# Unread products of the identity with itself in eleven waits of TensorE

## The chip, the cores and the metric

One core of one Trainium2 chip runs the whole program. The metric is the device time in microseconds, as the median of several executions; lower is better. The reference is a function of 34 arrays; all arithmetic is done on the core.

## The reference, cut to what matters

2048 tokens of width 256 pass through two residual blocks. The first is a gated linear-recurrence attention followed by an MLP of width 1024; the second is a mixture of 8 experts (two per token) with a shared expert of width 704.

```python
x = x + layernorm(attn(layernorm(x), ...))
x = x + layernorm(ffn(layernorm(x), ...))

def attn(x, ...):
    h = layernorm(x)
    x_conv = silu(causal_depthwise_conv(h, 4 taps))
    q, k = l2norm(h @ Wq), l2norm(h @ Wk)          # by heads of 16
    v = layernorm(h @ Wv)
    i_gate, gamma = sigmoid(x_conv @ Wig + big), sigmoid(x_conv @ Wg + bg)
    mem = scan(mem = gamma * mem + i_gate * k * v)    # over the tokens
    out = layernorm(layernorm(mem) * q) * gnw + gnb
    out = out * sigmoid(x_conv @ Wog + bog)
    h = x + out @ Wo
    h2 = layernorm(h)
    return h + (silu(h2 @ Wgate) * (h2 @ Wval)) @ Wout
```

Everything is fp32; the products of the MLPs are formed from high and low parts of each operand, three products each (`mm3`).

## The kernel before

The tokens are cut into four blocks (`TILES`) of four tiles of 128. Each block goes through the attention steps of the list `ATTENTION`, through the MLP (`mup`, `mdn`) and the shared expert (`hid`, `sdn`); the routed experts come at the end in 39 groups, then the final sum. Each engine has its own stream of instructions. `steps(engine)` merges two lists for it: `ORDER`, the steps of the MLPs and the router, and the attention steps, each of which stands before the element of `ORDER` whose number `PLACE[engine]` gives. The order is thus written out by hand, and each engine runs it in program order, with semaphores for what one engine needs from another. The attention of block b+1 is laid between the MLP steps of block b.

Two stretches have no MLP products beside them. One is the attention of block 0: all its steps stand ahead of the first `mup`. The other is the stop between the MLP of block 0 and that of block 1: after the last `mdn` of block 0 come `og`, `wo`, `ht` (of block 2, one block ahead), `xt`, `h2`, `route` and `logit`, and only then the first `mup` of block 1.

The steps of TensorE that the change touches, as (stage, block, part):

- `ut`: eight transposes of the update u to the layout by features. It waits for the vector engine's L1294.
- `mt`: eight products with the centring matrix, which also turn the scanned memory back to tokens. It waits for the scan, L1305.
- `g` part 2: the output gate's four products of 512 columns. It waits until the normalised memory has left `p_main` (L1333). ScalarE reads its result at L607.
- `og`: eight transposes of the output `HN`. It waits for L1336 and for the output gate.
- `wo`: the eight products with Wo. It waits for L1349, which itself follows ScalarE's L621 on the result of `og`.
- `ht` of the next block: eight transposes of the normalised input, after L1355 has read the result of `wo` from `p_main`.
- `h2`: eight transposes of the input of the MLP, two for each of four tiles that ScalarE writes at L632.
- `q` part 0 of the next block: four products with the weights of q, k and v. It waits for L637 on the result of `h2`.
- `xt`: eight transposes of the router's input, two for each of four tiles that ScalarE writes at L658.

`p_main` is banks 0 and 1 of PSUM, which these steps share one after the other. Bank 2 is the first bank of the first of two pairs (`p_pair`) that hold the halves of `mup` and `hid`. In the first block's attention `q` of block 0 uses it too (`q_banks`).

In fp32 one product on TensorE is recorded as two MATMULs with two weight loads; a transpose is recorded as one.

Of the kernel before, what the change touches and what calls it, by code (L numbers as in the profile page):

```python
# [11 lines left out]
P = 128  # L12
# [55 lines left out]
def _order():  # L68
# [89 lines left out]
    ],  # L158
}


def steps(engine):
# [9 lines left out]
def build(nc, x, wq, wk, wv, wig, wog, wo, wg, wgate, wval, wout, vecs, headvecs, router, sup, sdn, rup, rdn, out):  # L172
    ctx = ExitStack()
    with ctx:
# [3 lines left out]
        def sb(name, shape, dt=F32):  # L178
            return ctx.enter_context(nc.sbuf_tensor(name, shape, dt))

        psum = ctx.enter_context(nc.psum_tensor("psum", [P, 8, 512], F32))
# [51 lines left out]
        with ExitStack() as first_names:  # L233
            wr, wg16, wmean, _, wgx = (first_names.enter_context(nc.sbuf_tensor(k, s, F32)) for k, s in (
                ("wr", [P, C, RP]), ("wg16", [P, C, HEADS]), ("wmean", [P, C, HEADS]),
                ("under_rupr", [P, E * C * GU - C * (RP + 2 * HEADS)]), ("wgx", [P, C, D])))
# [7 lines left out]
        ident = sb("ident", [P, P])  # L244
# [497 lines left out]
        def _(pe):  # L742
# [6 lines left out]
            def to_features(dst, src, nj, ready=None, before=0):  # L749

                for j in range(nj):
                    if ready is not None:
                        pe.wait_ge(ready, before + j + 1)
                    for c in range(C):
                        last = nc.tensor.transpose(dst[:, c, j * P:(j + 1) * P], src(j)[:, c * P:(c + 1) * P], ident[:, :])  # L755
                return last
# [33 lines left out]
            def at(stage, b, m):  # L790
                nj, old, new = TILES[b], START[b], START[b + 1]
                tb = nj * P
                if (stage, m) == ("ht", 0):
                    if b > 0:
                        pe.wait_ge(hr_ready, b)
                    to_features(p_main, lambda j: QKV[:, j, 0:D], nj, hn_ready, old).then_inc(ht_psum, 1)
                if stage == "q" and m < nj:
# [12 lines left out]
                    for part, cols in ((0, slice(0, 2 * D)), (1, slice(2 * D, 3 * D))):  # L810
                        for c in range(C):
                            last = nc.tensor.matmul(q_banks(b, m)[:, part, 0:cols.stop - cols.start], HT[:, c, tok], WQKV[:, c, cols],  # L812
                                                    start=c == 0, stop=c == C - 1)
                    last.then_inc(qkv_psum, 1)
                if stage == "g":
# [8 lines left out]
                    for o in range(C):  # L824
                        if m == 1:
                            pe.wait_ge(gate_ready, C * 3 * b + o + 1)
                        for c in range(C):
                            if m == 1:
                                last = nc.tensor.matmul(p_main[:, o, 0:tb], wgx[:, c, o * P:(o + 1) * P], XC[:, c, 0:tb],  # L829
                                                        start=c == 0, stop=c == C - 1)  # L830
                            else:
                                cols = slice(m // 2 * D + o * P, m // 2 * D + (o + 1) * P)
                                last = nc.tensor.matmul(p_main[:, o, 0:tb], GW[:, c, cols], XC[:, c, 0:tb],  # L833
                                                        start=c == 0, stop=c == C - 1)
# [19 lines left out]
                if stage == "wo":  # L854
# [3 lines left out]
                    for j in range(nj):  # L858
                        cols = slice(j * P, (j + 1) * P)
                        for c in range(C):  # L860
                            last = nc.tensor.matmul(p_main[:, j // 2, (j % 2) * D:(j % 2 + 1) * D], OG[:, c, cols], WO[:, c, :],  # L861
                                                    start=c == 0, stop=c == C - 1)
# [44 lines left out]
                if stage == "rank":  # L907
# [6 lines left out]
                                     stop=False, skip_group_check=True)  # L914
# [15 lines left out]
            for name, b, m in steps("pe"):  # L930
                at(name, b, m)
# [619 lines left out]
```

## Time and profile before

| | |
|---|---|
| time, median of 3 runs | 600.58 us (600.44, 600.58, 602.94) |
| profiled execution, first to last instruction | 603.1 us |
| mean granted clock of TensorE | 0.933 |
| TensorE, MATMUL busy | 518.9 us, 86% of the span, 2408 instructions |
| VectorE, ScalarE, GpSimd busy | 394.2, 263.7, 109.5 us |

The profile's table of forty slices gives the busy share of each engine and the granted clock of TensorE in tenths. The chain of waits is followed back from the last instruction, and says which engine's work set the end. The timeline of an engine lists its instructions, with the idle time before each group and the instruction that ended it in square brackets. Times on the timeline are counted from the first instruction. The table by windows gives the granted clock of chosen stretches: 1.00 is 2.4 GHz and 0.50 is 1.2 GHz. The span is 0.2 us longer than the slowest of the three timed runs and 2.5 us longer than their median.

### The profile page before, as it was taken

Reading aid. Unit: us, or ns where it says so; the run is one execution under the profiler, and the core shown is the slowest. Engines: PE = TensorE matmul, PEld = TensorE weight load, DVE = VectorE, ACT = ScalarE, POOL = GpSimd, SP = SyncE. Lnnn points to the kernel's source line nnn. Section 1 sums busy time; section 2 is a strip of 40 time slices with the busy share of each in tenths; the row PEclk is TensorE's granted clock in tenths of the full one; section 3 lists DMA queues with packets and bytes.
Section 4 is the critical chain, followed back from the end, with each engine's and each line's share of the span. In section 5 each row is a group of like instructions: output and inputs, shape, how many; then the busy total and the mean of one; then the engine's idle time right before and its main releaser. Section 6 shows DMA issues by size and latency. Waiting matters only on the chain.

```text
span 603.1 us, 7985 instructions
## 1 busy us (share of the span) xinstructions
PE 518.9 (86%) x2408; PEld 407.6 (68%) x2408; DVE 394.2 (65%) x1159; ACT 263.7 (44%) x469; POOL 109.5 (18%) x133
## 2 busy tenths in 40 slices
PE   2845358999569999999999998999997899999981
PEld 1413234677446587886677786788876799999871
DVE  6786643879865798875497774434657666767236
ACT  4721444425374424276631444311344456666204
POOL 1510003200002323002204000050004034444300
PEclk9985679999959999999999999999989999999986
DMA  8950000001110002021001011010129234444364
GB/s 292 380 178 15 20 2 0 1 2 35 35 35 1 0 19 89 4 66 36 1 5 67 1 35 36 0 70 2 36 71 281 77 94 119 136 124 117 106 226 139
DMA packets 29547, 44.52 MB, mean 74 GB/s; under 512 B 3083, under 2 KB 24203, under 8 KB 29163
## 3 DMA queue, kind: packets, MB, share of 16 engines
q1 hardware_dynamic: 24515, 33.07, 17.8%
q0 software_dynamic: 3408, 9.38, 4.2%
q10 hardware_dynamic: 1584, 1.57, 0.9%
q8 instruction: 21, 0.34, 0.2%
q14 instruction: 19, 0.16, 0.1%
HBM read 27.67 MB, written 16.34 MB: 73 GB/s over the span
## 4 chain that ended last, share of the span: by engine, by line
PE 71%; DVE 15%; ACT 7%; DMA 4%; issue 2%; POOL 0%; ACTq 0%; POOLq 0%; SPq 0%; DVEq 0%
PE psum L786 14%; PE psum L745 12%; PE psum L746 11%; PE psum L747 11%; PE psum L812 5%; PE psum L755 4%; PE psum L833 3%; DMA RDNR<-rdn 2%; PE psum L861 2%; DVE XC L1244 2%; PE psum L829 2%; PE psum L847 2%; PE psum L986 1%; PE psum L956 1%; PE psum L939 1%
## 5 line engine op out<-in xcount | busy, mean ns | idle before, releaser
L650 ACT ACTIVATE SM<-psum 128x512 f32<-128x512 f32 (+1 forms) x56 | 33.2, 594 | 123.0 <-PE psum L747 99.7
L1369 DVE TENSOR_TENSOR SM<-SM,psum 128x512 f32<-128x512 f32 (+1 forms) x56 | 38.2, 683 | 56.4 <-ACT SM L650 56.3
L526 POOL DMA_INDIRECT x_dispatched<-XN,dest x32 | 32.5, 1017 | 159.2 <-DVE XN L1437 150.7
L786 PE MATMUL psum<-WOU,SM 128*128 128x256 f32 x256 | 60.2, 380 | 0.0
L786 PEld LDWEIGHTS psum<-WOU,SM 128*128 128x128 f32 x256 | 48.3, 190 | 10.7 <-issue 2.4
L517 POOL TENSOR_TENSOR OG<-QKV,hvec 128x256 f32<-128x256 f32 x16 | 13.4, 836 | 228.1 <-ACT IG L592 214.5
L812 PE MATMUL psum<-WQKV,HT 128*128 128x512 f32 (+1 forms) x128 | 47.5, 520 | 6.5 <-ACT QKV L585 3.1
L535 POOL DMA_INDIRECT y_routed<-GO,g_dest x39 | 37.8, 968 | 67.8 <-ACT GO L720 67.5
L786 PE MATMUL psum<-SDN,SM 128*128 128x256 f32 (+1 forms) x192 | 44.8, 382 | 0.0
L812 PEld LDWEIGHTS psum<-WQKV,HT 128*128 128x128 f32 x128 | 24.9, 201 | 28.0 <-issue 21.6
L786 PEld LDWEIGHTS psum<-SDN,SM 128*128 128x128 f32 (+1 forms) x192 | 35.9, 189 | 6.5 <-issue 1.3
L833 PE MATMUL psum<-XC,GW 128*128 128x512 f32 x64 | 31.6, 641 | 8.1 <-DVE HN L1333 5.9
L745 PE MATMUL psum<-H2H,wgtH 128*128 128x512 f32 x64 | 30.8, 481 | 0.0
L745 PE MATMUL psum<-RUPH,GXH 128*128 x78 | 28.9, 371 | 1.9 <-DVE GXL L1451 1.9
L755 PE MATMUL psum<-ident,QKV 128*128 128x128 f32 x64 | 11.2, 331 | 22.3 <-ACT QKV L563 9.2
L833 PEld LDWEIGHTS psum<-XC,GW 128*128 128x128 f32 x64 | 13.0, 206 | 22.5 <-issue 13.1
L745 PE MATMUL psum<-XTH,supH 128*128 128x512 f32 x66 | 27.8, 421 | 0.0
L1451 DVE TENSOR_TENSOR GXL<-psum,GXH 128x256 fp32r<-128x256 f32 x39 | 16.5, 424 | 15.7 <-ACT GXH L707 15.7
L747 PE MATMUL psum<-XTH,supL 128*128 128x512 f32 x66 | 26.2, 396 | 0.0
L746 PE MATMUL psum<-XTL,supH 128*128 128x512 f32 x66 | 26.0, 394 | 0.0
L746 PE MATMUL psum<-H2L,wgtH 128*128 128x512 f32 x64 | 25.8, 403 | 0.0
L747 PE MATMUL psum<-H2H,wgtL 128*128 128x512 f32 x64 | 25.8, 403 | 0.0
(295 smaller groups left out, 1301.4 us busy)
## 6 DMA issues: line engine op xcount, KB each, us to landing
XG<-x_dispatched SPq DMA_DIRECT2D x39, 130.0 KB, 2.7
YF<-y_routed SPq DMA_DIRECT2D x4, 1024.0 KB, 9.0
RUPR<-rup SPq DMA_DIRECT2D x1, 2816.0 KB
X<-x SPq DMA_DIRECT2D x4, 512.0 KB, 6.8
x_after_attention<-X SPq DMA_DIRECT2D x4, 512.0 KB, 2.9
QKV<-x ACTq DMA_DIRECT2D x3, 512.0 KB, 3.5
y_shared<-SH SPq DMA_DIRECT2D x3, 512.0 KB, 2.9
SHF<-y_shared SPq DMA_DIRECT2D x1, 1536.0 KB, 18.9
```

Of the source, the lines that this page charges most:

```text
L526: nc.gpsimd.indirect_dma_start(XD[:, :], bass.IndirectOffsetOnAxis(dest[:, i, old + j:old + j + 1], 0), XN[:, j, :], None).then_inc(dispat ...
L535: nc.gpsimd.indirect_dma_start(YD[:, :], bass.IndirectOffsetOnAxis(g_dest[:, i:i + 1], 0), GO[:, i % ORING, :], None).then_inc(go_kept[i % ...
L650: nc.scalar.activation(SM[0:rows, g % 3, 0:tb], p_pair(n)[0][0:rows, 0:tb], ACT.Silu).then_inc(silu_ready, 1)
L745: nc.tensor.matmul(dst, aH, bH, start=start, stop=False, skip_group_check=shared)
L746: nc.tensor.matmul(dst, aH, bL, start=False, stop=False, skip_group_check=shared)
L747: return nc.tensor.matmul(dst, aL, bH, start=False, stop=stop, skip_group_check=shared)
L755: last = nc.tensor.transpose(dst[:, c, j * P:(j + 1) * P], src(j)[:, c * P:(c + 1) * P], ident[:, :])
L786: last = nc.tensor.matmul(p_down[:, j // 2, (j % 2) * D:(j % 2 + 1) * D], SM[0:rows, g % 3, j * P:(j + 1) * P], weight[0:rows, m, :], star ...
L812: last = nc.tensor.matmul(q_banks(b, m)[:, part, 0:cols.stop - cols.start], HT[:, c, tok], WQKV[:, c, cols], start=c == 0, stop=c == C - 1)
L833: last = nc.tensor.matmul(p_main[:, o, 0:tb], GW[:, c, cols], XC[:, c, 0:tb], start=c == 0, stop=c == C - 1)
L1369: nc.vector.tensor_tensor(SM[0:rows, g % 3, 0:tb], SM[0:rows, g % 3, 0:tb], value_rows(n, rows)[:, 0:tb], ALU.mult).then_inc(hid_ready, 1)
L1451: nc.vector.tensor_tensor(GXL[:, i % 2].rearrange("p c t -> p (c t)"), g_bank(0, i)[:, 0:D], f32(GXH[:, i % 2].rearrange("p c t -> p (c t) ...
```

## The change

A table names eleven steps of TensorE and a count for each. Ahead of the step's own waits and work, TensorE now runs that many products of `ident` with itself, 128 by 128 by 128 in fp32, into the first 128 columns of bank 2. Each of them starts a new accumulation, and nothing reads the result. They wait for nothing. There are 157 of them in all: 115 in the attention of block 0 and its end (`ut`, `mt`, `g` part 2, `og`, `wo`, `ht` of block 1, `h2`, `q` of block 1), and 42 in the stop (`ht` of block 2, `xt`, `h2` of block 1). No other instruction, order or wait is changed.

```diff
+BUSY = {("ut", 0, 0): 17, ("mt", 0, 0): 16, ("g", 0, 2): 24, ("og", 0, 0): 26, ("wo", 0, 0): 9, ("ht", 1, 0): 5, ("h2", 0, 0): 12,
+        ("q", 1, 0): 6, ("ht", 2, 0): 27, ("xt", 0, 0): 8, ("h2", 1, 0): 7}
+
+
 def steps(engine):
 
@@ -790,6 +794,8 @@
             def at(stage, b, m):
                 nj, old, new = TILES[b], START[b], START[b + 1]
                 tb = nj * P
+                for _ in range(BUSY.get((stage, b, m), 0)):
+                    nc.tensor.matmul(psum[:, 2, 0:P], ident[:, :], ident[:, :], start=True, stop=True)
                 if (stage, m) == ("ht", 0):
```

## Rows read from the trace of the kernel before

**Rows 1.** The profile's page: granted clock in forty slices, and the chain by engine.
```profile
PEclk9985679999959999999999999999989999999986
PE 71%; DVE 15%; ACT 7%; DMA 4%; issue 2%; POOL 0%; ACTq 0%; POOLq 0%; SPq 0%; DVEq 0%
```
**Rows 2.** Windows of TensorE: stretch and length, busy (count), granted clock, DMA share, GB/s.
```profile
78.10:84.80 6.70, 2.12 (x13) 1.00 0.01 1
91.70:163.30 71.60, 64.19 (x261) 1.00 0.03 8
163.40:183.80 20.40, 13.05 (x43) 0.50 0.16 52
371.10:375.70 4.60, 1.97 (x16) 1.00 0.32 114
```
**Rows 3.** Timeline of TensorE, block 0: start, length, line, tiles, count, idle before.
```profile
27.50 3.70 PE L833 MATMUL psum<-XC,GW 128*128 128x512 f32 x8 [2.19 <-ACT QKV L585]
...
40.16 1.75 PE L755 MATMUL psum<-ident,QKV 128*128 128x128 f32 x8 [4.54 <-DVE QKV L1294]
45.85 3.78 PE L847 MATMUL psum<-centring,IG 128*128 128x128 f32 x16 [3.94 <-DVE IG L1305]
55.53 6.37 PE L833 MATMUL psum<-XC,GW 128*128 128x512 f32 x8 [5.90 <-DVE HN L1333]
68.61 1.97 PE L755 MATMUL psum<-ident,HN 128*128 128x128 f32 x8 [6.72 <-DVE HN L1336]
72.94 6.19 PE L861 MATMUL psum<-WO,OG 128*128 128x256 f32 x16 [2.35 <-DVE OG L1349]
80.44 1.09 PE L755 MATMUL psum<-ident,QKV 128*128 128x128 f32 x8 [1.31 <-DVE HR L1355]
84.99 2.08 PE L755 MATMUL psum<-ident,HN 128*128 128x128 f32 x8 [3.46 <-ACT HN L632]
88.70 4.28 PE L812 MATMUL psum<-WQKV,HT 128*128 128x512 f32 x8 [1.63 <-ACT GA L637]
```
**Rows 4.** Timeline of TensorE, both clocks: start, length, line, count.
```profile
45.85 2.50 PE L847 MATMUL psum<-centring,IG 128*128 128x128 f32 x10 [3.94 <-DVE IG L1305]
...
106.17 0.58 PE L745 MATMUL psum<-H2H,wgtH 128*128 128x512 f32 x1
...
109.16 3.60 PE L833 MATMUL psum<-XC,GW 128*128 128x512 f32 x8
...
123.98 2.05 PE L847 MATMUL psum<-centring,IG 128*128 128x128 f32 x16
125.78 0.48 PE L745 MATMUL psum<-H2H,wgtH 128*128 128x512 f32 x1
...
155.33 3.72 PE L861 MATMUL psum<-WO,OG 128*128 128x256 f32 x16 [0.53 <-DVE OG L1349]
```
**Rows 5.** The chain that ended last, block 0: start, length, what.
```profile
58.12 3.50 DMA QKV<-x
...
93.35 1.43 DVE XC L1244 x2
```
**Rows 6.** Timeline of ScalarE: the four tiles that `h2` turns.
```profile
84.25 2.08 ACT L632 ACTIVATE HN<-HR,l2n,l2r 128x256 f32<-128x256 f32 x4 [1.17 <-DVE l2n L1063]
```
**Rows 7.** Timeline of TensorE in the stop.
```profile
166.23 1.97 PE L755 MATMUL psum<-ident,QKV 128*128 128x128 f32 x8 [7.18 <-DVE HR L1355]
170.28 2.16 PE L755 MATMUL psum<-ident,XN 128*128 128x128 f32 x8 [2.08 <-ACT XN L658]
174.20 2.07 PE L755 MATMUL psum<-ident,HN 128*128 128x128 f32 x8 [1.75 <-ACT HN L632]
...
180.03 0.80 PE L745 MATMUL psum<-H2H,wgtH 128*128 128x512 f32 x1
...
184.64 2.74 PE L812 MATMUL psum<-WQKV,HT 128*128 128x512 f32 x8
```
**Rows 8.** Timeline of TensorE at the end of the third block.
```profile
372.67 1.09 PE L755 MATMUL psum<-ident,XN 128*128 128x128 f32 x8 [1.66 <-ACT SH L690]
```

## The prediction

> **What bounds the kernel now.** Read the page's chain by engine first: TensorE carries 71% of it [rows 1]. Then the granted clock in forty slices: full almost everywhere, but at 5 to 8 tenths early on, once near a quarter of the span, and at the very end [rows 1]. Windows place this: between 163.4 and 183.8 the clock is at 0.50, which is 1.2 GHz, while the MLP stretch from 91.7 to 163.3 runs at 1.00, 2.4 GHz [rows 2]. Third, TensorE's timeline in the two stretches without MLP work: short groups, each behind a wait for VectorE or ScalarE of 1.3 to 7.2 us [rows 3, 7]. These waits are a serial chain through two or three engines, and the change does not shorten them. What it can shorten are TensorE's own links in the chain, which run at the lower clock because the engine was idle before them: the `wo` products take 6.19 us at low clock and 3.72 at high [rows 3, 4], the centring products 3.78 and 2.05 [rows 3, 4].
>
> **What is added.** 157 products, each two MATMULs of 128 columns. At low clock ten centring MATMULs take 2.50 us and sixteen 3.78 [rows 3, 4], so one more costs 1.28/6 = 0.213 and a product 0.43 us. At high clock sixteen of them fill 123.98 to 125.78 [rows 4], 0.1125 each, 0.225 a product. Against the waits of [rows 3, 7], at high clock:
>
> - `ut` 17: 3.83 of 4.54; `mt` 16: 3.60 of 3.94; `g` 24: 5.40 of 5.90; `og` 26: 5.85 of 6.72
> - `wo` 9: 2.03 of 2.35; `ht` 5: 1.13 of 1.31; `h2` 12: 2.70 of 3.46; `q` 6: 1.35 of 1.63
> - stop: `ht` 27: 6.08 of 7.18; `xt` 8: 1.80 of 2.08; `h2` 7: 1.58 of 1.75
>
> Every one fits, with 0.2 to 1.1 us left, so at high clock all 35.3 us of them cost nothing: the wait that hides them is still the later event. If that cover goes (low clock) each costs twice as much and ten of the eleven overrun. They write a bank that nobody holds then, and queue no DMA. `ut` is the first, and its cover begins at high clock: the engine had been running gate products, and a wait of 2.19 us before them [rows 3] had not cost the clock.
>
> **Do such products hold the clock?** No row has identity times identity. The nearest is [rows 2, 8]: between 371.1 and 375.7 TensorE ran only 16 transposes, 1.97 us busy in 4.60, with the identity as moving operand, and the clock stayed at 1.00. The added products leave at most 1.1 us of any wait idle, less than waits through which the clock stayed (2.19 and 1.66 [rows 3, 8]), so they should hold it. The Trainium skill says otherwise of a neighbour: "TensorE: Matmul & The Clock Gate", Part 4 (PE-mode transpose), has the full clock not engage for transposes, which do not count as busy in the same way. By that rule the row just named would have lost the clock, and it did not. If the rule held, the clock would fall where transposes lie thick, which is the third case below.
>
> **Block 0, what each link gives at high clock.**
> - `ut`: 1.75 against 1.09 for eight transposes at high clock [rows 3]: 0.66. `mt`: 3.78 to 2.05 [rows 3, 4]: 1.73.
> - `g` part 2: 6.37 against 3.60 [rows 3, 4], but worth 0. Behind it VectorE works on without it, and in the chain stands the load of x, 3.50 us from 58.12 [rows 5]; ScalarE's squares come free before VectorE needs them. The `og` wait ends at the same distance from `g` as before.
> - `og`: 1.97 to 1.09: 0.88. `wo`: 6.19 to 3.72: 2.47. `ht`: already fast, 1.09.
> - `h2`: ScalarE delivers its four tiles over 2.08 us, until 86.33 [rows 6]; TensorE ends at 87.07 [rows 3]. The last tile's two transposes cannot start sooner; at high clock they end some 0.44 after it, so 0.3 is won, not 1.
> - `q` and the first `mup`: worth 0. What releases the next `q` is the convolution on VectorE, until 94.8 [rows 5], and ScalarE behind it; TensorE only waits longer.
>
> Sum 6.04.
>
> **The stop.** `ht` 1.97 to 1.09: 0.88; ScalarE's next tiles follow its result directly. `xt` and `h2` are paced by ScalarE like the `h2` above, 0.3 each. `mup`: its 12 products take 4.61 (180.03 to 184.64 [rows 7]) against 2.99 (106.17 to 109.16 [rows 4]): 1.62, and behind it TensorE is itself the bound. Sum 3.10. Both together 9.1.
>
> **What is late next: the `og` wait.** Once `g` part 2 runs at high clock it ends 2.77 sooner, and the `og` wait grows from 6.72 to 9.49. The 26 products cover 5.85 of it and leave 3.64 us idle. At high clock the waits of 3.46, 4.54, 6.72 and 7.18 us [rows 3, 7] all ended with the transposes behind them wholly or mostly at low clock; those of 2.19 and 1.66 [rows 3, 8] did not. So I expect the clock to fall here. Then `og` takes up to 1.97, and the nine products ahead of `wo` up to 9 x 0.43 = 3.84 where 2.35 is free: `wo` starts up to 1.49 later. `wo` itself runs fast: TensorE is then busy for up to 5.8 us without a pause, and the clock came back within 5.2 us of the start of `wo` at 72.94 [rows 2, 3]. The price is 0 (it holds) to 0.88 + 1.49 = 2.4; I take 1.6, since the clock may be back before the nine are done.
>
> 9.1 - 1.6 = 7.5. From the profiled execution's 603.1 that is 595.6. The median is 2.5 below the profile; part of that may be time at low clock in these same stretches, which cannot be saved twice. Of 0 to 2.5 I take half, 1.3: 600.58 - 7.5 + 1.3 = **594.4**, with an own range of 592.5 to 596.5.
>
> **Rivals.**
> 1. *The clock holds through the `og` wait too.* For it: nothing but chance in where the idle falls; against it the four rows above. 600.58 - 9.1 + 1.3 = 592.8. Chance 0.13.
> 2. *The forecast, and the clock falls a second time in the run of transposes*: `xt` and `h2` are paced at two transposes in 0.52 us, so TensorE is idle half the time there between the added products. Then `route` and most of the first `mup` are slow again: the stop gives 1.6 less, 596.0. For it: at 78.1 to 84.8 [rows 2] 13 MATMULs in 6.7 us ended in a fall. Against it: [rows 2, 8]. Chance 0.15.
> 3. *The gain is mostly not passed on*: a stall behind the first `mup` of block 1, or low stretches later on that move about, take it back. TensorE's 71% of the chain [rows 1] speaks against it. A quarter of 9.1 left, 2.3: 598.3. Chance 0.1.
> 4. *Slower: the products do not count as activity*, for example since nearly all their operands are zeros. All run at low clock and overrun: `ut` 7.3 for 4.54, +2.7; `mt` 6.8 for 3.94, +2.9; `g` and `og` together 10.2 + 6.4 + 11.1 after the release of `g`, where `og` started after 13.1, +8.6; `wo` +1.5; `ht` and `h2` +3.3; in the stop 11.5 for 7.18, 3.4 for 2.08 and 3.0 for 1.75, +6.9. Sum 26: 626. It decides from the first wait on: if the clock is at 0.50 when `ut` runs, this is the case. [Rows 8] speak against it. Chance 0.07.
>
> **How the numbers follow.** The forecast has 0.55, and 594.4 is its number. What this kernel's measurement tells from no change is about 0.5%, 3 us. Faster by more than that, below 597.6: forecast, rivals 1 and 2, and a little of 3: 0.85. Within 597.6 to 603.6: most of rival 3: 0.08. Slower: rival 4, 0.07. The range of 591.2 to 598.5 holds rivals 1 to 3 and both ends of the unknown terms; outside stand rival 4, the tail of 3, and a run that had all of 9.1 off the median: about 2 in 10.
>
> **What would show it.** Granted clock 1.00 from the first `ut` to the end of `g` part 2, with `mt` at 2.05 and `g` at 3.6; an idle stretch of about 3.6 ahead of `og` and a drop there; `wo` at 3.7; in the stop `ht` at 1.1 and twelve `mup` products in 3.0. In each wait an idle rest of 0.2 to 1.1 still ended by the same instruction as before. An added group that ends after its releaser, or a clock below 1.00 in the first two waits, would make the prediction wrong.

## The result, and the profile after

| | before | after |
|---|---|---|
| median of 13 runs each, us | 601.08 (600.11 to 603.92) | 595.61 (593.98 to 600.95) |
| ratio, 95% interval | | 0.990 [0.988, 0.992] |
| profiled execution: span, mean granted clock | 603.1, 0.933 | 592.7, 0.985 |

The change makes the kernel 1.0% faster. The forecast was 594.4 in a range of 591.2 to 598.5. Lines of the kernel after stand four to six further down than before (L786 is L790, L812 is L818, L833 is L839, L847 is L853, L861 is L867, L755 is L759); L798 is the added product.

The profile's page after, clock in forty slices, chain by engine and the group of the added products (busy us, mean ns), against [rows 1]:
```profile
PEclk9999899999999999999999999999999999999897
PE 73%; DVE 14%; ACT 7%; DMA 3%; issue 2%; POOL 0%; ACTq 0%; SPq 0%; DVEq 0%; POOLq 0%
...
L798 PE MATMUL psum<-ident 128*128 128x128 f32 x314 | 37.5, 278 | 0.0
```
Of the early slices that showed 5 to 8 one 8 is left; at the end there are still an 8 and a 7. 157 products are 314 MATMULs, 37.5 us of new work, nearly all of it inside waits.

Windows of TensorE after (length, busy, granted clock), against [rows 2]:
```profile
27.70:66.00 38.30, 32.75 (x214) 1.00 0.34 113
66.20:69.40 3.20, 2.90 (x14) 0.50 0.00 0
69.60:472.20 402.60, 381.08 (x1741) 1.00 0.12 38
```
One drop is left in the whole part that the change touches, at 66.1, and the next comes at 472.3.

Timeline of TensorE after, block 0, against [rows 3]:
```profile
35.63 3.96 PE L798 MATMUL psum<-ident 128*128 128x128 f32 x34
40.33 1.09 PE L759 MATMUL psum<-ident,QKV 128*128 128x128 f32 x8 [0.74 <-DVE QKV L1300]
41.27 3.74 PE L798 MATMUL psum<-ident 128*128 128x128 f32 x32
45.37 2.05 PE L853 MATMUL psum<-centring,IG 128*128 128x128 f32 x16 [0.37 <-DVE IG L1311]
47.26 5.52 PE L798 MATMUL psum<-ident 128*128 128x128 f32 x48
53.32 3.70 PE L839 MATMUL psum<-XC,GW 128*128 128x512 f32 x8 [0.54 <-DVE HN L1339]
56.86 5.97 PE L798 MATMUL psum<-ident 128*128 128x128 f32 x52
66.50 1.97 PE L759 MATMUL psum<-ident,HN 128*128 128x128 f32 x8 [3.67 <-DVE HN L1342]
68.25 2.78 PE L798 MATMUL psum<-ident 128*128 128x128 f32 x18
70.87 3.64 PE L867 MATMUL psum<-WO,OG 128*128 128x256 f32 x16
75.83 1.09 PE L759 MATMUL psum<-ident,QKV 128*128 128x128 f32 x8 [0.20 <-DVE HR L1361]
80.39 1.82 PE L759 MATMUL psum<-ident,HN 128*128 128x128 f32 x8 [0.78 <-ACT HN L636]
83.84 2.82 PE L818 MATMUL psum<-WQKV,HT 128*128 128x512 f32 x8 [0.29 <-ACT GA L641]
...
91.32 2.85 PE L818 MATMUL psum<-WQKV,HT 128*128 128x512 f32 x8 [1.87 <-ACT QKV L589]
```
Read the brackets: each group still waits for the instruction that released it before, for 0.2 to 0.8 us where it was 1.3 to 6.7. The exception is `og`: ahead of it 3.67 us stay idle and the clock falls. The nine products ahead of `wo` (x18) fill its whole wait, and just overrun it: VectorE has written `OG` at 70.67 and `wo` starts at 70.87, 0.06 later behind it than where the products leave a rest (0.14 us, in the kernel with 42 products below). The second part of `q` starts at 91.32 where it started at 96.18; the 0.17 by which this execution was late at 40.33 counted, block 0 gives 5.0.

The stop after, against [rows 7]:
```profile
154.03 6.19 PE L798 MATMUL psum<-ident 128*128 128x128 f32 x54
161.40 1.10 PE L759 MATMUL psum<-ident,QKV 128*128 128x128 f32 x8 [1.17 <-DVE HR L1361]
162.33 1.95 PE L798 MATMUL psum<-ident 128*128 128x128 f32 x16
164.58 1.91 PE L759 MATMUL psum<-ident,XN 128*128 128x128 f32 x8 [0.30 <-ACT XN L662]
166.33 1.73 PE L798 MATMUL psum<-ident 128*128 128x128 f32 x14
168.24 1.81 PE L759 MATMUL psum<-ident,HN 128*128 128x128 f32 x8 [0.19 <-ACT HN L636]
...
173.60 0.50 PE L749 MATMUL psum<-H2H,wgtH 128*128 128x512 f32 x1
...
176.50 2.74 PE L818 MATMUL psum<-WQKV,HT 128*128 128x512 f32 x8
```
From the first transposes to the `q` behind the first `mup` it takes 15.10 us where it took 18.41 [rows 7]: 3.3.

### The profile page after: what moved, and what is told of

The parts are those of the page before. It is cut to its first block, busy times and chain, and to the rows that moved or that the text cites. A ratio compares the mean times of both kernels' runs of the same rounds, so it can differ in the third digit from the quotient of the medians.

```text
span 592.7 us, 8613 instructions
## 1 busy us (share of the span) xinstructions
PE 539.4 (91%) x2722; PEld 433.9 (73%) x2722; DVE 393.9 (66%) x1159; ACT 264.1 (45%) x469; POOL 109.8 (19%) x133
## 4 chain that ended last, share of the span: by engine, by line
PE 73%; DVE 14%; ACT 7%; DMA 3%; issue 2%; POOL 0%; ACTq 0%; SPq 0%; DVEq 0%; POOLq 0%
PE psum L790 15%; PE psum L749 12%; PE psum L751 11%; PE psum L750 11%; PE psum L818 6%; PE psum L839 3%; PE psum L759 3%; PE psum L992 3%; DMA RDNR<-rdn 2%; PE psum L835 2%; PE psum L867 2%; PE psum L962 1%; DVE XC L1250 1%; PE psum L945 1%; PE psum L853 1%
## 5 line engine op out<-in xcount | busy, mean ns | idle before, releaser
L790 PE MATMUL psum<-WOU,SM 128*128 128x256 f32 x256 | 60.2, 380 | 0.0
L790 PEld LDWEIGHTS psum<-WOU,SM 128*128 128x128 f32 x256 | 48.2, 189 | 10.9 <-issue 2.4
L818 PE MATMUL psum<-WQKV,HT 128*128 128x512 f32 (+1 forms) x128 | 46.9, 516 | 6.6 <-ACT QKV L589 4.6
L818 PEld LDWEIGHTS psum<-WQKV,HT 128*128 128x128 f32 x128 | 24.8, 200 | 27.4 <-issue 19.3
L790 PE MATMUL psum<-SDN,SM 128*128 128x256 f32 (+1 forms) x192 | 44.8, 381 | 0.0
L790 PEld LDWEIGHTS psum<-SDN,SM 128*128 128x128 f32 (+1 forms) x192 | 35.8, 189 | 6.6 <-issue 1.3
L798 PEld LDWEIGHTS psum<-ident 128*128 128x128 f32 x314 | 37.0, 195 | 1.1 <-issue 1.0
L798 PE MATMUL psum<-ident 128*128 128x128 f32 x314 | 37.5, 278 | 0.0
L839 PE MATMUL psum<-XC,GW 128*128 128x512 f32 x64 | 29.0, 595 | 2.0 <-ACT QKV L589 1.5
L751 PE MATMUL psum<-RUPH,GXL 128*128 x78 | 25.8, 331 | 0.0
L750 PE MATMUL psum<-RUPL,GXH 128*128 x78 | 25.8, 331 | 0.0
```

The costliest lines, as they stand in the source:

```text
L750: nc.tensor.matmul(dst, aH, bL, start=False, stop=False, skip_group_check=shared)
L751: return nc.tensor.matmul(dst, aL, bH, start=False, stop=stop, skip_group_check=shared)
L790: last = nc.tensor.matmul(p_down[:, j // 2, (j % 2) * D:(j % 2 + 1) * D], SM[0:rows, g % 3, j * P:(j + 1) * P], weight[0:rows, m, :], star ...
L798: nc.tensor.matmul(psum[:, 2, 0:P], ident[:, :], ident[:, :], start=True, stop=True)
```

## The experiments

My theory: what the change wins is the faster clock on TensorE's links of the chain and nothing else, so each stretch pays by itself, a wait left idle loses it, and products beyond a wait cost their full time. One run of each kernel was traced, and it need not be the typical one. The times beside are of the kernel before on the same chip, which had medians of 602.35, 603.29 and 602.37 in the three sessions; kernels of different sessions are best compared by ratio.

**Block 0 alone, and the stop alone.**
```diff
-        ("q", 1, 0): 6, ("ht", 2, 0): 27, ("xt", 0, 0): 8, ("h2", 1, 0): 7}
+        ("q", 1, 0): 6}
```


> The change in block 0's attention alone: 115 products, the three entries of the stop (ht of block 2, xt, h2 of block 1) left out. Clock theory: each stretch pays by itself. The first q of block 1 after its part 0 starts 4.5 to 5.0 us earlier than before (about 91.3 instead of 96.2), the stop is as it was (waits of 7.2, 2.1 and 1.8 us, clock 0.50, about 13.4 us from its first transposes to the mup of block 1), and the time is 600.8 minus 4.5, about 596.3, that is 1.5 to 3.3 above the whole change. Rival (what the first stretch wins is given back at the next wait that is not TensorE's): the first mup of block 1 starts where it did and the time is above 599.

Measured: 596.97 against 602.35, ratio 0.990 [0.987, 0.993]. The stop is slow as before. The traced run is the slowest of seven (600.71), and in it the second part of `q` starts at 92.58 and not at 91.32, though up to there the kernel is the changed one. TensorE, then the window:
```profile
66.32 1.97 PE L759 MATMUL psum<-ident,HN 128*128 128x128 f32 x8 [3.66 <-DVE HN L1342]
...
71.92 3.84 PE L867 MATMUL psum<-WO,OG 128*128 128x256 f32 x16
...
92.58 4.54 PE L818 MATMUL psum<-WQKV,HT 128*128 128x512 f32 x8 [1.86 <-ACT QKV L589]
```
```profile
65.60:72.20 6.60, 5.88 (x27) 0.50 0.00 0
```
Here the clock stayed low longer, until all nine products ahead of `wo` were done: `wo` starts 5.60 us after `og`, where it was 4.37. It fell again at 92.8, behind the wait of 1.86 that had passed without a fall in the trace above, and that part of `q` took 4.54 us instead of 2.85. What the same instructions and nearly the same waits cost differs between executions.
```diff
+BUSY = {("ht", 2, 0): 27, ("xt", 0, 0): 8, ("h2", 1, 0): 7}
```


> The change in the stop alone: 42 products. Clock theory: block 0 as before (centring products 3.8 us, wo 6.2 us at clock 0.50), the stop at 1.00 with twelve mup products in 3.0 instead of 4.6 us, 3.1 to 3.3 us saved: about 597.6. Together with the other half the two savings add up to the whole change within 1 us. Rival (halves overlap or the median's gain is chance of the phase): the two savings add to more than 8 or less than 4 us.

Measured: 600.35 against 602.35, ratio 0.997 [0.995, 0.999]. The gains of 5.4 and 2.0 add to 7.4; the whole change won 5.5 above and 6.8 in a later session (below). That agrees with halves that add up, but does not show it: block 0 alone has the whole change's ratio, 0.990, so the times do not resolve what the stop adds to it, though alone it gives something. Block 0 carries most. The stop gave less than its 3.3. Its trace, of the slowest of twelve runs (602.69), shows one thing that can take it back. TensorE in the stop of this kernel, then the window:
```profile
178.78 0.41 PE L905 MATMUL psum<-ident,SH 9*128 9x9 f32 x4 [1.80 <-ACT SH L676]
179.11 0.50 PE L749 MATMUL psum<-H2H,wgtH 128*128 128x512 f32 x1
...
183.56 2.74 PE L818 MATMUL psum<-WQKV,HT 128*128 128x512 f32 x8
```
```profile
179.90:183.20 3.30, 3.30 (x9) 0.50 0.00 0
```
With all three waits filled the clock fell all the same, after the wait of 1.80 ahead of `logit`, and the twelve products took 4.45 us instead of 2.90. This wait was 0.68 us in the kernel before; it grew once `route` ran fast. The price is that of the prediction's second rival, the place is not: that one put the fall in the run of transposes. It comes in some executions only: of the ten traces with the stop filled in full, three show it (this one and those of the kernels with the seven products alone and with `hid` alone, below). Why the median won only 2.0 stays open, since the other eleven runs were not traced.

**Products enough for the `og` wait.**
```diff
-("og", 0, 0): 26
+("og", 0, 0): 42
```


> The whole change with 42 instead of 26 products ahead of og, so that they cover the 9.6 us that this wait has once the output gate runs at high clock (42 x 0.2235 = 9.4). Clock theory: the one drop in this part of the trace (66.1 to 69.5, og at 1.97 us) is gone; og takes 1.09, wo starts 3.44 us after og instead of 4.37, and the time is 0.9 to 1.5 us below the changed kernel, about 594.5. Rival (the drop costs nothing, since the nine products ahead of wo and the wait hide it): same time within 0.3. Rival (42 overrun the wait): og starts later than 13.1 us after the release of the output gate, and the time is above the changed kernel's.

Measured: 594.52 against 602.35, ratio 0.987 [0.985, 0.990]. TensorE around `og`:
```profile
56.69 9.54 PE L798 MATMUL psum<-ident 128*128 128x128 f32 x84
66.34 1.09 PE L759 MATMUL psum<-ident,HN 128*128 128x128 f32 x8
67.27 2.17 PE L798 MATMUL psum<-ident 128*128 128x128 f32 x18
69.79 3.69 PE L867 MATMUL psum<-WO,OG 128*128 128x256 f32 x16 [0.35 <-DVE OG L1355]
```
`wo` starts 3.45 us after `og`, where it was 4.37: the drop cost 0.92 in that trace, 0.86 of it in `og` and what follows up to `OG`, 0.06 in the overrun. By the same measure it cost 2.15 in the trace of block 0 alone. No drop is left before 437.2 in this trace, of the fastest of six runs; two other kernels with 42, alike up to there, show drops (at 90.7 and 176.0, and at 174.1). By the intervals the time alone does not tell 42 from 26. The 9.6 us wait is filled to within a tenth without delaying `og`.

**Transposes in place of products.**
```diff
-                for _ in range(BUSY.get((stage, b, m), 0)):
-                    nc.tensor.matmul(psum[:, 2, 0:P], ident[:, :], ident[:, :], start=True, stop=True)
+                for _ in range(2 * BUSY.get((stage, b, m), 0)):
+                    nc.tensor.transpose(psum[:, 2, 0:P], ident[:, :], ident[:, :])
```


> The whole change with each added product replaced by two transposes of the identity by the identity (314 in all, one MATMUL each, so the same count of MATMULs of 128 columns). From the trace, where a stretch of nothing but transposes kept the clock: transposes hold the clock like products, all waits filled as before, time equal to the changed kernel's within 0.5, clock 1.00 from ut to the output gate. Rival (the Trainium skill, TensorE: Matmul & The Clock Gate, Part 4, where transposes do not count as busy): the clock is 0.50 from ut on, the added work runs at half speed and overruns the waits, ut + 2.7, mt + 2.9, output gate and og + 8.6 and so on, about 26 us above the kernel before, 626.

Measured: 596.11 against 602.35, ratio 0.990 [0.987, 0.994], the same as the change. Windows:
```profile
35.70:67.00 31.30, 25.64 (x203) 1.00 0.17 50
67.20:70.40 3.20, 3.20 (x17) 0.50 0.00 0
```
In the first stretch nearly all of the 203 instructions are transposes or products of 128 columns, and most are transposes of an identity; the clock stays. The Trainium skill ("TensorE: Matmul & The Clock Gate", Part 4, PE-mode transpose) has transposes not engage the full clock. This trace, of fp32 transposes, does not agree, and the measurement decides.

**No products ahead of `og`.** The entry `("og", 0, 0): 26` is left out.

> The whole change without its 26 products ahead of og. Clock theory: they leave 3.7 us idle anyway, so the clock falls there with them or without; without them it falls earlier, and og (2.0 us) and the nine products ahead of wo (3.84 in a free 2.35) run wholly at low clock. wo starts 5.8 us after og instead of 4.4, and the time is 0.5 to 1.5 above the changed kernel. Rival (the 26 carry the gain of all that follows): wo at 6.2 us, ht and h2 slow as before, 4 us lost.

Measured: 597.45 against 603.29, ratio 0.989 [0.985, 0.992]: the time does not tell it from the change. The trace does:
```profile
66.35 1.97 PE L759 MATMUL psum<-ident,HN 128*128 128x128 f32 x8 [9.46 <-DVE HN L1342]
68.11 3.74 PE L798 MATMUL psum<-ident 128*128 128x128 f32 x18
71.69 3.62 PE L867 MATMUL psum<-WO,OG 128*128 128x256 f32 x16
```
`wo` starts 5.34 us after `og`, 1.89 more than with 42. With 26 (in one trace 52 transposes in their place) the four traces have 4.34, 4.37, 4.56 and, in block 0 alone, 5.60. So the 26 products left `wo` earlier in three traces of four; that a wait filled by 60% is worth anything on average is not shown.

**All counts doubled.**
```diff
-                for _ in range(BUSY.get((stage, b, m), 0)):
+                for _ in range(2 * BUSY.get((stage, b, m), 0)):
```


> The whole change with all eleven counts doubled (314 products). If each added product costs 0.2235 us from the point where its wait is full: ut + 3.1, mt + 3.2, output gate and og + 6.9, wo + 1.7, ht and h2 of block 0 + 1.8, q 0, stop: ht + 4.9, xt + 0.6, h2 + 0.5, no drop of the clock (- 0.9): 22 us above the changed kernel, about 617, at clock 1.00 throughout. Rival (TensorE would have idled anyway and the overrun is hidden by other engines): less than 10 us above.

Measured: 614.17 against 603.29, ratio 1.018 [1.014, 1.023]. Timeline:
```profile
43.27 1.04 PE L759 MATMUL psum<-ident,QKV 128*128 128x128 f32 x8
...
51.28 1.95 PE L853 MATMUL psum<-centring,IG 128*128 128x128 f32 x16
53.07 10.88 PE L798 MATMUL psum<-ident 128*128 128x128 f32 x96
63.79 3.60 PE L839 MATMUL psum<-XC,GW 128*128 128x512 f32 x8
67.23 11.78 PE L798 MATMUL psum<-ident 128*128 128x128 f32 x104
78.84 1.04 PE L759 MATMUL psum<-ident,HN 128*128 128x128 f32 x8
```
None of these groups has a wait in brackets any more. `ut` is 2.9 later than in the changed kernel, `mt` 5.9, the gate 10.5, `og` 12.3; the `q` behind the first `mup` of block 1 starts at 196.49 against 176.50, 20.0 later, where I expected 22. By ratio the time is 2.8% above the change's, some 17 us. The clock is at 1.00 until 468.8. So a full clock is no gain in itself: beyond its wait each product costs what it takes.

**Only the six longest waits filled.**
```diff
+BUSY = {("ut", 0, 0): 17, ("mt", 0, 0): 16, ("g", 0, 2): 24, ("og", 0, 0): 42, ("h2", 0, 0): 12, ("ht", 2, 0): 27}
```


> The kernel with 42 products ahead of og, and those ahead of five short waits (wo, ht of block 1, q, xt, h2 of block 1: 1.3 to 2.4 us) left out; only the six waits of 3.5 us and more are filled. Clock theory: a single short wait does not lose the clock, so block 0 keeps wo at 3.7 us and the q of block 1 starts where it did; in the stop two short waits and two groups of transposes paced by ScalarE follow each other, the clock falls in between, and route and mup are slow: 1.6 to 2 us above the kernel with 42, about 596.5. Rival (every wait needs its products): wo and h2 in block 0 are slow too, 4 us above. Rival (none of the short ones matters): same time within 0.3.

Measured: 597.71 against 603.29, ratio 0.990 [0.986, 0.993], where 42 products with the short waits filled had 0.987: within the intervals, so the trace must decide. Timeline:
```profile
70.16 5.20 PE L867 MATMUL psum<-WO,OG 128*128 128x256 f32 x16 [2.35 <-DVE OG L1355]
76.68 1.10 PE L759 MATMUL psum<-ident,QKV 128*128 128x128 f32 x8 [1.32 <-DVE HR L1361]
...
84.68 5.46 PE L818 MATMUL psum<-WQKV,HT 128*128 128x512 f32 x8 [1.63 <-ACT GA L641]
92.92 2.74 PE L818 MATMUL psum<-WQKV,HT 128*128 128x512 f32 x8
```
My expectation of block 0 was wrong. The clock fell at 69.8, in a wait of 2.35 us right behind `og`, and `wo` took 5.20; it fell again at 83.5, ahead of `q`, which took 5.46, and now the second part of `q` has no wait: it starts at 92.92 against 90.30. In the stop the clock fell as I had expected, from 165.4 on. In this trace the short waits needed their products too; whether they do in each execution is not shown.

**Four more waits, the first expert product alone, and `hid` alone.** All have 42 ahead of `og`. The first has 7 ahead of `logit`, 9 each ahead of two `hid` steps and 7 ahead of the first expert product; the second only those last 7; the third only those of `hid`.
```diff
+                for _ in range({("hid", 3, 3): 9, ("hid", 3, 4): 9}.get((stage, b, m), 0)):
+                    nc.tensor.matmul(psum[:, 0, 0:P], ident[:, :], ident[:, :], start=True, stop=True)
...
                 if stage == "up":
+                    for _ in range(7 if i == 0 else 0):
+                        nc.tensor.matmul(psum[:, 2, 0:P], ident[:, :], ident[:, :], start=True, stop=True)
```


> The kernel with 42 products ahead of og, and products in four more waits: 7 ahead of logit in the stop (1.80 us free), 9 each ahead of the fourth and fifth hid step of block 3 (2.2 to 2.3 free, not the same in each execution), 7 ahead of the first expert product (1.89 free). Clock theory: of the low stretches that are left (near 437, 451, 471 us, 3.4 us each, which come and go) two are gone and each gave 1.0 to 1.7, less up to 0.5 where hid's wait is shorter than its products: 1 to 2.5 us below the kernel with 42, about 592.5. Rival (those stretches lie over work that waits for others, so nothing is won): same time within 0.5.

> 42 products ahead of og and 7 ahead of the first expert product, nothing ahead of logit and hid. From the traces so far: the expert groups took 84.1 us from the first expert product to the final sum with these 7 and 85.6 without; the products ahead of hid gave nothing, since ScalarE waited there for the load of the experts' down weights. Expected: 1.4 us below the kernel with 42 alone, about 2.4 below the changed kernel on the same chip, and equal to the kernel with products in four more waits within 0.5. Rival (the 7 only move the low stretch elsewhere): first expert product to final sum at 85.5, same time as with 42 alone.

> 42 products ahead of og and 9 each ahead of the fourth and fifth hid step of block 3. Transfer theory: ScalarE stands behind the load of the experts' down weights (issued near 439, landed near 452), and releases the fifth step; so the clock there is worth nothing, the first transposes of the expert groups start no earlier than with 42 alone (468.7), and the time is that of 42 alone within 0.5 or above it. Rival (clock): 1 to 1.7 us below.

Measured: 592.98 against 603.29, ratio 0.984 [0.980, 0.988]; 593.70 against 602.37, ratio 0.985 [0.982, 0.987]; 596.47 against 602.37, ratio 0.990 [0.987, 0.993]. From the first expert product to the final sum the kernel with 42 alone took 85.6 us and the two with the seven products 84.1 and 84.0. The third, without the seven, took 85.5. The start of that stretch in the first of these, then in the kernel with 42 alone:
```profile
470.95 1.73 PE L953 MATMUL psum<-ident 128*128 128x128 f32 x14
473.00 0.42 PE L749 MATMUL psum<-RUPH,GXH 128*128 x1 [0.33 <-DVE GXL L1461]
```
```profile
471.28 0.62 PE L749 MATMUL psum<-RUPH,GXH 128*128 x1 [1.89 <-DVE GXL L1457]
```
All twelve traces without the seven products have a drop of the clock within 1.4 us of that start, the two with them none. The `hid` products won nothing. ScalarE's first split of the experts' weights, in the kernel with 42 alone:
```profile
451.53 1.38 ACT L687 ACTIVATE RUPH<-RUPR 128x1408 fp32r<-128x1408 f32 x1 [6.31 <-DMA RDNR<-rdn]
```
It stands behind a load there, in the kernel with four more waits too (8.48 us), and the fifth `hid` step stands behind ScalarE. The kernel with 42 alone had two drops there (437.3 to 440.5 and 450.9 to 454.2) and was hardly late for it: from the `q` of block 2 to the first expert transposes it took 293.3 us, the changed kernel with no drop there 292.9. The first and the second kernel of this group settle it: from the `q` after that one both took 289.4, with the drops at 440.3 and 454.0 in the second and none there in the first. Where a transfer ends the wait, the clock is worth next to nothing.

**The changed kernel again, and half the counts.** The second divides every entry by two, rounded down.

> The changed kernel itself, beside the others on one chip: 5.5 to 6.5 us below the kernel before, one drop of the clock ahead of og, whose price in wo's start is 0.9 to 2.4 us depending on where it falls.

> The changed kernel with all counts halved (76 products), so that each wait is filled to about 45% and up to 4.9 us of it stay idle. Clock theory: idle rests of 2.2 us and more in mt, the output gate, og, h2 and ht of block 2 lose the clock as often as in the kernel before in the longer ones; the time lies halfway, 597.5 to 599 where the kernel before has 601 to 603. Rival (any activity in each wait is enough): within 0.5 of the changed kernel.

Measured: 595.56 against 602.37, ratio 0.990 [0.987, 0.994]; and 600.26, ratio 0.997 [0.994, 0.999]. Half the work in each wait brings about a third of the gain, less than the half that I expected (597.5 to 599). Its trace has waits of 2.76, 3.22, 5.16 and 4.30 us left, and the clock fell once at each. But it is of the fastest of twelve runs, which spread from 596.1 to 602.8; the others have a lower mean clock, 0.957 to 0.973 against 0.979.

The best kernels tried are the two with the seven products ahead of the first expert product, at 0.984 and 0.985 of the time before; the change has 0.990.

## Why the prediction was right

- *What the products cost.* 0.225 us each at high clock: 48 MATMULs took 5.52 us and 84 took 9.54, so one more product takes 0.223. The rests that I gave (0.71, 0.34, 0.50 for `ut`, `mt`, `g`) were measured at 0.74, 0.37 and 0.54.
- *They hold the clock.* Shown: 1.00 from 27.7 to 66.0, and rival 4 falls. Doubled, they even held it to 468.8. But the row that I leaned on [rows 2, 8] was luck: in five of the thirteen later traces the clock fell in that same stretch of transposes, between 363.1 and 371.0, and from the second `q` behind the stop to the first expert transposes those five took 0.8 to 2.4 us more than the others. And at low clock all eleven groups would overrun the waits listed, not ten.
- *Block 0.* `mt` 2.05, `g` 3.70, `wo` 3.64, and the last two `h2` transposes bound by ScalarE, as said. That `g` and the first `q` are worth nothing holds too: `og` starts 13.2 us after `g` where it was 13.1, and the second part of `q` sits 1.87 us waiting for ScalarE where it had 0.4.
- *The `og` wait.* I expected 3.64 us idle and a drop; it was 3.67 and a drop, in the trace and in its repeat. The term for it, 1.6 of a possible 2.4, was too large for this trace: 0.92 by the kernel with 42, with the 0.88 for `og` as forecast and the overrun at 0.06, since the clock was back before the nine products were done (they took 2.78, not 3.84). In the trace of block 0 alone they took 4.05 and the price was 2.15. Over the four traces with 26 it is 0.9, 0.9, 1.1 and 2.15, so the range was right and 1.6 no bad guess.
- *The stop.* 3.10 forecast, 3.3 in the trace. But rival 2, to which I gave 0.15, is not an alternative to the forecast. Something of its price happens in a part of the executions, three of ten traces, and makes the next `mup` 1.5 to 1.6 later each time. It came behind the wait ahead of `logit`, which the sum passed over, and not in the run of transposes.
- *From the trace to the median.* This is the step that was off. The traces differ by 10.4 us, the touched stretches by 8.1, the medians by 5.5. I set the profile 2.5 above the median and took off 1.3. But a span is not a time: after, a span of 592.7 belongs to a run of 594.48, 1.8 more, and with the same 1.8 the profile before stands near 604.9 (an estimate), above all 13 of its runs. Nor is either trace typical: the mean clock after, 0.985, is the highest of its 13 runs (two at 0.971 took 600.27 and 600.95 us), and the 0.933 before is below all 45 later runs of that kernel (0.934 to 0.943). 2.3 of the 10.4 lies behind the touched stretches: from the start of the last sum to TensorE's end 25.1 us before and 22.6 after. A drop fell there in both, but before it slowed the last 64 products (15.77 us against 13.98), which had already waited 2.17 for the load of the expert outputs. The forecast of 7.5 for the trace erred low by 0.6 where it applied, and the correction for the median should have been 2 to 2.6 and not 1.3. The sum is off by 1.2 us; 0.5 of that is the starting value, 600.58 of three runs where 13 have 601.08. That the number came so near owes something to errors that offset each other. How much of the rest is drops that come and go in the other runs of both kernels is open; the traces of block 0 alone and of the three stops show such drops at 1.2 to 1.6 us each.

## What to carry to other kernels

Where TensorE's short links stand in a serial chain with other engines, unread products in its waits keep them at full clock in most executions; count them from the wait as it will be once the link before has become fast, not as it is (26 were right for a wait of 6.72 that turned into 9.6). Fill the short waits too, also those that appear once a link has become fast (0.68 us ahead of `logit` turned into 1.80), and stop short of the releaser: from there each product costs its whole time. Before filling a wait, look at what ends it: behind a transfer the clock buys next to nothing. And compare two traces stretch by stretch: the same instructions kept the clock in one execution and lost it in another.

## What the runs showed of the hardware

- 314 transposes of the identity by itself hold TensorE at 2.4 GHz as well as 157 fp32 products do (596.1 and 595.6 us).
- A wait of 2.35 us, with 1.1 us of transposes and 0.3 us idle before it, cost the clock (0.50 from 69.8 to 73.2), though in the changed kernel rests of 1.87 us and less passed without a drop in block 0.
- The same wait does not always end the same way: the 1.87 us ahead of the second part of `q` kept the clock in the changed kernel's two traces and lost it in those of block 0 alone and of `hid` alone (0.50 from 92.8 and from 90.7; eight products took 4.54 us, not 2.85).
- Seven products (1.7 us) ahead of the first expert product save 1.5 us in the 85 behind it: no drop there in two traces with them, one in each of twelve without.
